# Adaptive-norm attention with a sparse feed-forward block: loads reordered, router sums turned, last score tiles in one pass, engine orders rewritten

## What is computed

```
mod = silu(c) @ wmod                      # six rows: sa, ca, ga, sb, cb, gb
h = layernorm(x) * (1 + ca) + sa
x = x + ga * (causal_attention(h) @ Wo + bo)          # one head of width 128
h = layernorm(x) * (1 + cb) + sb
prob = softmax(h @ w_router + b_router)   # 16 blocks, the best 4 are kept
y = relu(h @ w1.T + b1), masked by block, @ w2.T + b2
x = x + gb * y
```

## Time and profile before

| | |
|---|---|
| median of 3 runs | 121.91 us (121.81 to 121.94) |
| profiled execution | 121.85 us |
| its span, first to last instruction | 120.1 us |
| granted TensorE clock, mean | 0.994 |
| busy PE / PEld / DVE / ACT / POOL | 111.9 / 90.7 / 89.4 / 76.4 / 90.4 us |
| chain that ended last: PE / DVE / POOL / DMA / issue / ACT | 66 / 12 / 5 / 5 / 4 / 3 % |

### The profile page before, as it was taken

How to read it: one execution, slowest core, us unless ns; L and a number is a source line. 1 busy time by engine, 2 the same in 40 slices (tenths; PEclk the granted TensorE clock), 3 DMA queues, 4 the chain that set the end, 5 groups by cost and what they waited for, 6 DMA issues and landing times.

```text
span 120.1 us, 2032 instructions
## 1 busy us (share of the span) xinstructions
PE 111.9 (93%) x606; PEld 90.7 (76%) x606; DVE 89.4 (74%) x305; ACT 76.4 (64%) x165; POOL 90.4 (75%) x125
## 2 busy tenths in 40 slices
PE   6979799999999999999999999999998999999770
PEld 2459577898888888888887888888886878867550
DVE  0479999999799999789895265942698745878931
ACT  2324979958782859595968988687632585536430
POOL 6787879974989999899769989999964688642000
PEclk9999999999999999999999999999999999999997
DMA  2894000000000000000000000000000000003053
GB/s 53 234 357 103 0 3 3 5 0 0 3 0 0 5 0 0 0 0 0 3 0 5 0 0 0 0 0 0 0 0 8 0 0 0 3 0 87 5 165 97
DMA packets 6273, 3.42 MB, mean 29 GB/s; under 512 B 1140, under 2 KB 5877, under 8 KB 6262
## 3 DMA queue, kind: packets, MB, share of 16 engines
q1 hardware_dynamic: 5830, 3.09, 9.0%
q10 hardware_dynamic: 432, 0.20, 0.6%
HBM read 2.24 MB, written 1.05 MB: 27 GB/s over the span
## 4 chain that ended last, share of the span: by engine, by line
PE 66%; DVE 12%; POOL 5%; DMA 5%; issue 4%; ACT 3%; POOLq 1%; DVEq 1%
PE bank L777 16%; PE bank L781 16%; PE bank L778 16%; PE bank L820 7%; PE bank L885 3%; DMA x<-in_L_attn_y_all_dram 3%; PE bank L801 2%; DVE hid_full L711 2%; POOL hid_lo L446 2%; DVE keys L688 2%; DMA out_dram<-res 2%; POOL rstd L368 2%; DVE xn L602 2%; PE bank L895 2%; ACT xn L509 1%
## 5 line engine op out<-in xcount | busy, mean ns | idle before, releaser
L440 POOL TENSOR_TENSOR p_lo<-p_full,p_hi 128x512 fp32r<-128x512 f32 (+3 forms) x40 | 45.3, 1155 | 6.6 <-ACT p_full L537 6.5
L530 ACT ACTIVATE p_hi<-bank 128x512 fp32r<-128x512 f32 (+3 forms) x40 | 21.5, 539 | 8.3 <-DVE bank L660 5.2
L537 ACT ACTIVATE p_full<-bank 128x512 f32<-128x512 f32 (+3 forms) x40 | 21.4, 536 | 3.3 <-POOL p_lo L440 3.3
L446 POOL TENSOR_TENSOR hid_lo<-hid_full,hid_hi 128x512 fp32r<-128x512 f32 x12 | 15.4, 1289 | 6.3 <-ACT hid_hi L553 6.3
L625 DVE TENSOR_REDUCE cmax<-bank 128x1 f32<-128x512 f32 x24 | 16.1, 686 | 1.0 <-PE bank L820 0.9
L820 PE MATMUL bank<-zt_hi,g_hi 128*128 128x512 f32 (+3 forms) x40 | 15.2, 392 | 0.3 <-DVE nmax L628 0.3
L553 ACT CAST hid_hi<-hid_full 128x512 fp32r<-128x512 f32 x16 | 9.8, 620 | 8.4 <-DVE hid_full L711 6.8
L777 PE MATMUL bank<-g_hi,zt_hi 128*128 128x512 f32 (+3 forms) x40 | 15.1, 377 | 0.1
L777 PE MATMUL bank<-p_hi,z_hi 128*128 128x512 f32 (+3 forms) x40 | 15.0, 376 | 0.0
L781 PE MATMUL bank<-p_lo,z_hi 128*128 128x512 f32 (+3 forms) x40 | 14.7, 367 | 0.1
L711 DVE SCALAR_TENSOR_TENSOR hid_full<-bank,keep 128x512 f32<-128x512 f32 x16 | 10.8, 687 | 5.0 <-POOL hid_lo L446 2.2
(11 more groups left out here) (167 smaller groups left out, 257.9 us busy)
## 6 DMA issues: line engine op xcount, KB each, us to landing
x<-in_L_attn_y_all_dram SPq DMA_DIRECT2D x4, 256.0 KB, 3.9
out_dram<-res SPq DMA_DIRECT2D x3, 256.0 KB, 2.4
w<-in_L_ffn_w_dram SPq DMA_DIRECT2D x2, 256.0 KB, 4.8
wmod<-in_L_wmod_dram SPq DMA_DIRECT2D x1, 256.0 KB, 4.6
out_dram<-res SPq DMA_DIRECT2D x2, 128.0 KB, 1.9
wmod<-in_L_wmod_dram ACTq DMA_DIRECT2D x1, 128.0 KB, 3.7
wk<-in_L_attn_Wk_dram SPq DMA_DIRECT2D x1, 64.0 KB, 3.3
wq<-in_L_attn_Wq_dram ACTq DMA_DIRECT2D x1, 64.0 KB, 3.5
```

The costliest lines, as they stand in the source:

```text
L440: pool.tensor_tensor(p_lo[:, s, w:], p_full[:, n % 2, w:], p_hi[:, s, w:].bitcast(F32), ALU.subtract).then_inc(p_lo_pool, 1)
L446: pool.tensor_tensor(hid_lo[:, m, :], hid_full[:, n % 2, :], hid_hi[:, m, :].bitcast(F32), ALU.subtract).then_inc(hid_lo_pool, 1)
L530: nc.scalar.activation(p_hi[:, s, w:], src, ACT.Exp).then_inc(p_hi_s, 1)
L537: nc.scalar.activation(p_full[:, n % 2, w:], src, ACT.Exp).then_inc(p_full_s, 1)
```

## The change

1. SP's loads: `w1` goes ahead of x of group 1, the second half of `wmod` ahead of x of group 2.
2. PE's setup: six of the fourteen zero matmuls go, the transposes of `w1` (z6) and the fold (z2) come ahead of n0; the router weights (z9) are made after a0 into a score bank, copied by ACT (`wr_full`), and split by POOL instead of DVE.
3. Constants that POOL made (`base`, `ident_r`, `ident_b`, ones, `back`, `nmax`, `keys`, most of `future`) are made by DVE ahead of the first statistics.
4. Last tiles (`whole(t)`, t = 3, 11, 23, 39): one exponential into `p_last`, one float32 matmul with `z_last` in place of three, no low half on POOL. POOL copies `z_last` once for each group.
5. Router of groups 0 to 2 (`SWUNG`): the weights are the stationary operand, two matmuls of 512 columns in place of eight of 32; DVE turns the 32-row result back in four 32x128 transposes, and ACT's copy of the mask reorders the tokens. Group 3 keeps eight matmuls, the four with `h_hi` first, in `score_bank[0]`.
6. Keys: one instruction over the group in place of four.
7. All four plans are rewritten.

```diff
-            load_x(1)
+            load(w1[:], w1_in.rearrange("(p m) d -> p m d", p=P), w1_in_s)
+            load_x(1)
+            load(wmod[:, 2 * D:], wmod_in[:, 2 * D:], mod2_in_s)
             load_x(2)
-            load(wmod[:, 2 * D:], wmod_in[:, 2 * D:], mod2_in_s)
-            load(w1[:], w1_in.rearrange("(p m) d -> p m d", p=P), w1_in_s)
...
+                if whole(t):
+                    nc.scalar.activation(p_last[:], src, ACT.Exp).then_inc(p_hi_s, 1)
+                    return
...
+                if whole(t):
+                    pe.wait_ge(p_hi_s, t + 1)
+                    mm(ctx_bank[:, w:], z_last[:, g, :], p_last[:], start=False, stop=True).then_inc(pv_done, 1)
+                    return
...
+                if g in SWUNG:
+                    for i in range(GT):
+                        last = nc.vector.transpose(swung_sums[Q * i:Q * i + Q].rearrange("p b s e -> p (b s e)"),
+                                                   norm_bank[0:Q, i * P:(i + 1) * P])
+                    step(last)
+                    sums = swung_sums[:]
...
-                for i in range(GT):
-                    last = nc.vector.tensor_scalar(keys[:, i, 0:NBLK], logit[:, i, :], lmax[:, i:i + 1], UNDER, ALU.subtract, ALU.max)
-                last.then_inc(keys_s, 1)
+                most = lmax[:].rearrange("p (i o) -> p i o", o=1).broadcast_to([P, GT, NBLK])
+                nc.vector.scalar_tensor_tensor(out=keys[:, :, 0:NBLK], in0=most, scalar=UNDER, in1=logit[:], op0=ALU.add,
+                                               op1=ALU.max).then_inc(keys_s, 1)
...
+                if g in SWUNG:
+                    pe.wait_ge(nt_hi_s, NG + g + 1)
+                    pe.wait_ge(nt_lo_s, NG + g + 1)
+                    if g == 0:
+                        pe.wait_ge(wr_s, 1)
+                    mm(norm_bank[0:Q, :], halves, grp(h_hi, g), start=True, stop=False)
+                    mm(norm_bank[0:Q, :], halves, grp(h_lo, g), start=False, stop=True).then_inc(logits_mm, 1)
+                    return
```

More of the change, by code:

```diff
@@ new lines @@
+a22 w7 a23 s11 w8 a24 w9 b2 w10 a25 w11 n4 a26 s12 a27 s13 a28 s14 a29 a30 s15 a31 w12 a32 s16 a33 w13 s17 o1
+s18 r0 s19 a34 s20 a35 w14 s21 a36 s22 w15 a37 w16 a38 w17 a39 w18 w19 s23 b3 h0 w20 w21 s24 w22 s25 w23 s26
+s27 m0 s28 w24 w25 n5 o2 s29 w26 s30 s31 h1 r1 s32 s33 w27 s34 h2 s35 m1 w28 w29 w30 s36 w31 n6 s37 w32 h3 s38
+r2 s39 w33 w34 w35 w36 w37 w38 w39 h4 m2 d0 o3 d1 d2 d3 h5 h6 d4 h7 y0 h8 d5 n7 d6 h9 r3 h10 d7 h11 d8 h12 m3
+d9 h13 d10 h14 d11 h15 y1 d12 d13 y2 d14 d15 d16 d17 d18 d19 y3 y4
@@ L52 @@
+m1 e34 h1 e35 n6 e36 e37 e38 h2 e39 h3 c3 h4 y0 m2 h5 h6 a7 h7 n7 h8 h9 h10 y1 h11 m3 h12 h13 h14 y2 h15 y3 y4
 """
 VECTOR_PLAN = """
[L54 to L57, removed]
+g0 z1 a0 g1 z3 g2 z10 n0 z11 g3 q0 s0 n1 s1 s2 s3 q1 s4 b0 s5 z5 s6 s7 n2 s8 s9 s10 s11 s12 b1 s13 s14 s15 s16
@@ L58 @@
+s17 s18 s19 n3 i8 q2 x0 i9 g4 s20 i10 s21 s22 s23 i11 s24 b2 s25 s26 s27 s28 s29 s30 s31 s32 s33 n4 z6 x1 g5
+s34 i20 s35 s36 i21 s37 i22 s38 s39 q3 i23 b3 m0 c0 h0 x2 n5 g6 m1 c1 h1 i36 h2 n6 i37 i38 m2 h3 i39 c2 h4 x3
+g7 h5 h6 h7 h8 n7 h9 m3 h10 c3 h11 f0 h12 h13 k12 h14 k13 h15 k14 k15 f1 f2 f3 f4
 """
 GPSIMD_PLAN = """
-z7 z0 z8 z5 p0 z1 z2 p1 u0 p2 z6 p3 u1 l0 l1 l2 l3 u2 l4 l5 l6 l7 z4 l8 u3 l9 l10 l11 z10 l12 l13 l14 l15 l16
-p4 l17 l18 p5 l19 l20 l21 l22 l23 z9 l24 l25 l26 l27 l28 l29 l30 l31 l32 p6 k0 l33 l34 k1 l35 k2 l36 l37 l38
@@ L103, in splits_to @@
     def splits_to(t, by_vector):
-        return sum(vector_splits(k) == by_vector for k in range(t + 1))
+        return sum(vector_splits(k) == by_vector and not whole(k) for k in range(t + 1))
     def scalar_applies(n):
@@ L375, in token_halves @@
                 pool.wait_ge(*norm_applied(g))
+                ahead(pool.tensor_copy(z_last[:, g, :], norm_rows(g)[:, GT - 1, :]))
                 step(pool.tensor_copy(tokens(z_hi, g), norm_rows(g)))
@@ L414, in prepare @@
                                        pattern=[[-1, P]], channel_multiplier=1).then_inc(causal_made, 1)
-                elif i == 2:
-                    step(pool.memset(back[:, P:P + 1], 0.0))
-                    pool.memset(back[0:1, P:P + 1], 1.0)
-                    pool.memset(xn2[:, :, :, 0:1], 1.0)
-                    pool.memset(nmax[:], 0.0).then_inc(ones_made, 1)
                 elif i == 7:
-                    step(pool.memset(future[:], 0.0))
+                    step(pool.memset(future[:, GW - P:], 0.0))
                     pool.affine_select(out=future[:, GW - P:], in_=future[:, GW - P:], compare_op=ALU.is_ge, fill=FAR, base=0,
@@ L696, in choose @@
                 for i in range(GT):
-                    last = nc.vector.match_replace(marked[:, i, :], top8[:, i, :], keys[:, i, :], 1.0)
+                    last = nc.vector.match_replace(marked[:, i, :], top8[:, i, :], keys[:, i, :], FURTHEST)
                 step(last)
@@ L889, in router @@
             def router(g):
+                halves = wr_halves[:].rearrange("p s e -> p (s e)")
+                if g in SWUNG:
+                    pe.wait_ge(nt_hi_s, NG + g + 1)
[5 more added lines that the diff above has]
+                    return
+                sums = [sums_bank(g)[:, i * 2 * NBLK:(i + 1) * 2 * NBLK] for i in range(GT)]
+                if g == NG - 1:
+                    pe.wait_ge(*score_free(TILES - 1))
+                    pe.wait_ge(nt_hi_s, NG + g + 1)
+                else:
+                    pe.wait_ge(nt_lo_s, NG + g + 1)
+                for i in range(GT):
+                    mm(sums[i], tile(h_hi, g * GT + i), halves, start=(i == 0), stop=False)
                 pe.wait_ge(nt_lo_s, NG + g + 1)
                 for i in range(GT):
-                    sums = norm_bank[:, i * 2 * NBLK:(i + 1) * 2 * NBLK]
-                    halves = wr_halves[:].rearrange("p s e -> p (s e)")
-                    mm(sums, tile(h_hi, g * GT + i), halves, start=True, stop=False)
-                    last = mm(sums, tile(h_lo, g * GT + i), halves, start=False, stop=True)
+                    last = mm(sums[i], tile(h_lo, g * GT + i), halves, start=False, stop=(i == GT - 1))
                 last.then_inc(logits_mm, 1)
```

94 lines of the change are left out of this document (58 added, 36 removed).

## The result

The changed kernel took **121.19 us** (median of 4 runs, 120.95 to 121.35), the kernel before beside it 121.90. The ratio is 0.994, with a 95% interval of 0.992 to 0.996: 0.6% faster, where 118.9 (2.5%) was predicted and the range ended at 117.9 and 120.8. The sign was right, the size was not. The profiled execution took 121.35 us, with a span of 119.3 (before 121.85 and 120.1). In some executions of every kernel here, the one before included, the granted clock of TensorE falls for a stretch of setup, which makes them up to 2.0 us longer, so from here on times are medians of the executions with a mean granted clock of at least 0.989, with their count in brackets.

A forecast was written before the change was run, and what follows sets the result against it. PE's list was taken to bound the kernel from about 19 to 110 us, with a load-to-query chain before and a second chain at the end. Terms summed to -3.0: 118.9 us against 121.91, range 117.9 to 120.8.

The forecast's parts named there:

- Setup and early part: Up to the first scores: moved PE setup and new POOL and DVE work cost +0.4 us, bounds -0.1 and +0.9.
- Router, weights, last tiles, order ahead of o3: PE's work up to o3: router groups 0 to 2 -1.4, router weights -0.2, last tiles +0.1, order -0.5 us.
- All in PE's full stretch: Routers of groups 0 to 2: the 1.4 us saved lies wholly where PE has no idle time.
- Waits between s0 and o3: PE's wait for POOL in group 3 goes, -0.25; a 0.1 to 0.5 wait at m2 replaces 0.61 before o3, -0.3.
- o3 to n7: From o3's start to n7's start: no change, 0, bounds -0.2 and +0.4 us.
- n7 to h12: Last group's router, keys and choice up to h12: -0.85 us, bounds -0.2 and -1.1.
- Behind h12: From h12 to the end of the span: left alone by the change, 12.1 us as before.
- The work goes, the time comes back as waits: Rival, 120.6 us, chance 0.22: DVE leads PE, savings become waits at b3 and m2, setup costs its full bound.
- The clock falls in setup: Rival, 122.8 us, chance 0.05: PE drops to half speed in setup as transposes replace zero matmuls.

The follow-up runs named there:

- e13: Changed kernel with all four routers back as eight short matmuls, none turned, keys in SBUF; 119.99 us.
- e12: Changed kernel with logits and marked keys in PSUM and all four routers as eight short matmuls, none turned; 119.47 us.
- e3: Changed kernel with the router's logits and marked keys in free PSUM columns instead of SBUF, same instructions and order; 119.34 us.
- e14: e11 with all four routers as eight short matmuls, none turned; 119.74 us.
- e11: e3 with the add of b1, still in SBUF, five row maxima earlier and m0 one score tile later; 118.76 us.
- e2: Changed kernel with the router of group 2 back as eight short matmuls, groups 0 and 1 still turned; 119.97 us.
- e9: Changed kernel run again unchanged, as reference; 121.27 us, ratio 0.994 to the kernel before.
- e15: e11 with SP's loads in the old order and the transposes of w1 behind those of w2; 118.69 us.

## Why the prediction was wrong, point by point

The span shrank by 0.8, where 3.0 was forecast.

- **Setup and early part, +0.4:** +0.58 at s0. In size about right. g_hi at 13.19 and n0 at 9.12 as forecast.
- **Router, weights, last tiles, order ahead of o3, together -2.0 of PE's work:** s0 to o3 fell from 72.03 to 71.23. Less the single waits over 0.15 us, listed in the next point, it fell from 70.9 to 69.0, -2.0. So the work was sized about right. "All in PE's full stretch" was the wrong step: PE's full rows up to b3 go at DVE's pace. By s0 to o3 the three turned routers cost 0.9 with all holds (e13 against the changed kernel), give 0.5 with the keys freed (e12 against e3), and 1.24 with the add of b1 freed and m0 later too (e14 against e11).
- **Waits between s0 and o3, -0.25 and -0.3:** they grew by 1.2: from 1.1 (0.24 at m0, 0.24 at the last tile, 0.61 ahead of o3) to 2.3 (0.28 at 51.60, 0.17 at 54, 0.33 at m0, 0.25 at the last tile, 1.23 at m2). This is the step that failed most. For DVE's steps from r2 to the end of the choice the prediction has 5.1 to 5.5 us, against 5.0 of PE's work; they took 6.4 (83.69, 0.23 behind the start of r2's second matmul, to 90.07), because the keys and the choice were held, and m2 waited 1.23 instead of 0.1 to 0.5. With the hold taken away (e3) they took 4.9 (83.73 to 88.63), and m2 waited 0.07. The kernel before shows the hold already, in all four groups (607 to 1465 ns below, 1.47 in group 2); the prediction didn't ask what made one instruction's durations differ so. The wait at the last tile changed its cause and not its size: 0.25, for a mask on DVE behind the held keys, instead of 0.24 for POOL. The add of b1, not in my sum at all, gave 0.45 at 51 and 54.

```profile
L702 DVE TENSOR_SCALAR chosen<-marked x4: 607/1246/1465, 63.2 to 105.6; 128x512 bf16<-128x512 f32 x4
```

- **o3 to n7, 0:** 7.64 for 7.76. Right.
- **n7 to h12, -0.85:** -0.47. The logits started 2.82 behind n7 (the forecast had the sums ready at 2.85, though the terms that it names, 0.41, 1.4 and 0.92, add up to 2.73) and the keys took 0.23 (0.3); the choice was held for 1.22. Without the hold: -0.99.
- **Behind h12, 0:** 12.1 both times. Right.
- **The rivals.** "The work goes, the time comes back as waits" was the right one, with three waits named (b3, setup, m2) and all three there; it gave 120.65 because it took the transposes' upper bound for the cause and knew nothing of the hold. The clock falls in setup: this isn't what made the changed kernel slower than forecast, since its profiled execution has full clock throughout. In e2's profiled execution it does fall, between 14 and 20 us (row below, columns as above, clock 0.72), but 9 of 23 executions of the kernel before on that chip are near 123.0 too, with a clock of about 0.98. On the chip of e9, the changed kernel has a clock under 0.989 in 2 of 12, the kernel before in 4 of 23. Nor does the Trainium skill's rule on transposes ("TensorE: Matmul & The Clock Gate", Part 4: PE-mode transpose) show in these counts.

```profile
14.00:20.00 6.00, 5.97 (x26) 4.56 (x26) 4.43 (x9) 4.22 (x12) 5.22 (x14) 0.72 0.00 1
```

## What to carry to other kernels

Where one line's instructions of one shape differ by a factor of two or three (here 607/1246/1465 ns before the change), don't price the next one at the shortest: lay their ends beside the ends of the other engines' instructions, and find what holds them. The sign here was a fixed distance: seven choices, all four before and three of four after, end 0.28 us behind the end of a POOL instruction, whenever they start. The distance differs from one instruction to another (the held keys end within 0.1, the held add of b1 0.9 behind). A source in PSUM set the choice free for 0.26 us. And a full PE row proves no lead: with DVE beside it at 90% (13.45 of 15 us), 71 and 77 matmuls took the same time.

The fastest kernel here is e15 (e11 is within 0.1 of it): keys in PSUM, the add of b1 where POOL is idle, m0 a tile later, loads and `w1` in the old order; 118.69 us against 122.03 beside it.

## What was not expected of the hardware

- The hold works the other way too. Behind the held add of b1, POOL's `p_lo` at 49.97 takes 2.02 us (the longest of the row below), where those of its shape before it take 1.29 to 1.31. It ends 1.16 us behind the end of the add. The three `p_lo` that start under a held choice (two before, one after) take 1.46 and end 1.14 behind it.

```profile
L452 POOL TENSOR_TENSOR p_lo<-p_full,p_hi x36: 737/1294/2018, 22.5 to 86.6; 128x512 fp32r<-128x512 f32 x28, 128x384 fp32r<-128x384 f32 x4, 128x256 fp32r<-128x256 f32 x4
```

- The hold isn't every POOL instruction's, against the rule on the port pair cited above. At 76.17 the changed kernel's choice took 0.43 us while POOL was in its power step (128x4, 75.43 to 76.63):

```profile
75.43 1.20 POOL L385 TENSOR_TENSOR rstd<-rstd,pow_half 128x4 f32<-128x4 f32 x1
...
76.17 0.43 DVE L730 TENSOR_SCALAR chosen<-marked 128x512 bf16<-128x512 f32 x1
```

- An add over one partition and 512 elements costs 1.06 us with one operand in PSUM and 1.07 with both in SBUF and POOL idle, where 128x512 from PSUM takes 0.68: the strided second operand, or the single partition, costs as much as the hold often does. Which of the two was not tried.
- Four 32x128 transposes on DVE take 1.27 us, 0.3 each, the upper bound of the prediction.
